# Paired groups of a graph layer: permuting message inputs in float32r instead of permuting f32 message rows

## The reference

```
h    = relu(layernorm(x))
msg  = concat(h[dst], edge_attr)                  # 53125 x 128
m    = relu(msg @ W1a.T + b1a) @ W1b.T + b1b
agg  = segment_sum(m, src) / max(count, 1)        # 3125 x 64
z    = relu(concat(h, agg) @ W2a.T + b2a) @ W2b.T + b2b
out  = x + concat(z, h) @ Wr.T + br
```

## Time and profile before

| | |
|---|---|
| median of 3 runs | 522.39 us (520.93 to 524.32) |
| profiled execution, first to last instruction | 518.3 us |
| median less span | 4.1 us, the start and end that the trace doesn't show |
| PE, DVE, ACT, POOL busy | 431.0, 298.0, 285.0, 356.1 us |
| indirect transfers issued by POOL | 300 + 64 |
| first and last of them | 14.06 us, 477.08 us |

### The profile page before, as it was taken

One profiled execution on the slowest core, in us unless ns is written; L12 is line 12 of the kernel. 1 busy time (PEld: TensorE's weight loads), 2 busy tenths in 40 slices (PEclk: granted clock), 3 DMA queues, 4 the chain that ended last, 5 costly groups with the idle time before them and its releaser, 6 DMA issues.

```text
span 518.3 us, 9203 instructions
## 1 busy us (share of the span) xinstructions
PE 431.0 (83%) x3133; PEld 390.0 (75%) x3133; DVE 298.0 (57%) x825; ACT 285.0 (55%) x576; POOL 356.1 (69%) x406
## 2 busy tenths in 40 slices
PE   6655988899999999998689779845999787987795
PEld 4555777888796988878578778845998777987674
DVE  7868642534656657555425547414765537667884
ACT  3442957774787777786658378171633772100073
POOL 4777777777677777777777777777777777776000
PEclk9876696987999899988899889986999897999999
DMA  7998998553959477978553989996999997778631
GB/s 182 306 338 229 257 266 271 155 156 108 303 143 294 141 257 265 257 255 263 164 151 92 336 249 333 312 331 196 360 326 336 328 322 221 248 214 256 177 86 43
DMA packets 62319, 123.45 MB, mean 238 GB/s; under 512 B 9369, under 2 KB 33374, under 8 KB 62270
## 3 DMA queue, kind: packets, MB, share of 16 engines
q1 hardware_dynamic: 49598, 91.25, 59.0%
q0 software_dynamic: 12672, 31.58, 18.8%
HBM read 71.53 MB, written 51.25 MB: 237 GB/s over the span
## 4 chain that ended last, share of the span: by engine, by line
POOL 32%; PE 26%; DMA 13%; issue 13%; DVE 7%; ACT 5%; SPq 2%; POOLq 0%; ACTq 0%; DVEq 0%
POOL slots_dram L568 24%; PE bank L1261 10%; POOL pairs_dram L551 8%; DMA slots_dram<-pay,pos_i 7%; PE bank L1241 4%; PE bank L1270 4%; DMA dstb<-in_dst 4%; DVE oh L774 2%; DMA rows<-slots_dram 2%; ACT eo L1059 2%; SPq L475 1%; PE bank L1294 1%; PE bank L1291 1%; PE bank L1211 1%; PE bank L1362 1%
## 5 line engine op out<-in xcount | busy, mean ns | idle before, releaser
L568 POOL DMA_INDIRECT slots_dram<-pay,pos_i x300 | 289.0, 963 | 98.7 <-issue 89.6
L1261 PE MATMUL bank<-rows,oh 128*125 128x130 f32 x1100 | 139.5, 287 | 40.3 <-DVE oh L774 40.1
L1261 PEld LDWEIGHTS bank<-rows,oh 128*125 128x125 f32 x1100 | 133.3, 198 | 44.6 <-issue 43.4
L1059 ACT ACTIVATE eo<-dstb,minus_lane 64x256 f32<-64x256 int32 x190 | 85.1, 494 | 94.5 <-DMA dstb<-in_dst 79.8
L1241 PE MATMUL bank<-pw,eo 128*128 128x128 f32 x856 | 119.9, 299 | 3.5 <-ACT pay L1042 2.3
L1241 PEld LDWEIGHTS bank<-pw,eo 128*128 128x128 f32 x856 | 113.3, 213 | 11.4 <-issue 8.0
L774 DVE TENSOR_TENSOR oh<-bank,rows 128x1500 f32<-128x1500 f32 (+5 forms) x67 | 81.8, 1223 | 17.6 <-DMA rows<-slots_dram 10.4
L1270 PE MATMUL bank<-hid,xch 116*128 116x131 f32 (+1 forms) x512 | 68.3, 294 | 14.6 <-DVE xch L724 8.6
L1270 PEld LDWEIGHTS bank<-hid,xch 116*128 116x128 f32 (+1 forms) x512 | 65.3, 205 | 16.9 <-issue 9.9
L551 POOL DMA_INDIRECT pairs_dram<-pay,pos_c x64 | 61.5, 960 | 22.3 <-issue 18.0
L1064 ACT ACTIVATE eo<-eo,one 64x512 f32<-64x512 f32 x95 | 68.3, 719 | 3.1
(11 more groups left out here) (198 smaller groups left out, 376.7 us busy)
## 6 DMA issues: line engine op xcount, KB each, us to landing
rows<-slots_dram SPq DMA_DIRECT2D x24, 864.0 KB
dstb<-in_dst SPq DMA_DIRECT2D x54, 256.0 KB, 7.7
eo<-in_edges_T SPq DMA_DIRECT2D x54, 256.0 KB, 4.9
rows<-pairs_dram SPq DMA_DIRECT2D x12, 864.0 KB
slots_dram<-zeros SPq DMA_DIRECT2D x9, 756.0 KB, 9.2
slots_dram<-pay,pos_i POOLq DMA_INDIRECT x300
rows<-slots_dram SPq DMA_DIRECT2D x8, 432.0 KB
rows<-slots_dram SPq DMA_DIRECT2D x16, 216.0 KB
```

Of the source, the lines that this page charges most:

```text
L568: pool.indirect_dma_start(out=slots_dram[:, :], out_offset=bass.IndirectOffsetOnAxis(ap=pos_i[:, u, k:k + 1], axis=0), in_=pay[:, u, k, :] ...
L1059: last = A.activation(eo[p, g % EB, a * HB:(a + 1) * HB], dstb[p, g % DB // 2, a * HB:(a + 1) * HB], ACT.Square, bias=minus_lane[p, g // 2 ...
L1261: last = T.matmul(o[0:BN, v * SW:(v + 1) * SW], oh2[:, r % 2, n, :], rows[:, sum_no[r] % RR, n, 0:SW], start=(t == 0), stop=(t == TB[ph] - ...
```

## The change

In a paired group nothing goes through `hidden` any more. Instead:

- SP loads the edge features of the group lane by lane (`edges_rows`, 116 x 512 floats, 237 KB) to `staged`; the 256 KB `dstb` broadcast, the `eo` load and the ACT one-hot of a paired group are gone.
- ACT rounds them to float32r (`round_features` to `x_hi`); DVE (`features`) writes mark, destination and a one-hot of `dst` over 62 nodes into `x_hi`, and the remainders to `x_lo`.
- DVE makes the slot one-hots by two instructions of 116 x 1024 a group instead of eight of 116 x 256.
- PE multiplies: stationary `x_hi` and `x_lo`, moving `perm`, all float32r, 16 matmuls of 256 columns a group, in two rounds "perm" of 8.
- ACT copies each half (`copy_moved`, 128 x 512) to `moved`; PE then makes the message rows of two edges per slot from it (`paired_hidden`, 8 f32 matmuls of 131 columns); ACT applies relu into `pay2` (`relu_unit`, 4 of 128 x 262).
- `pos_c` is read from `pay2` as before, at a later point of DVE's list (`places_due`).
- `chunk_marks` and `late_lanes` also clear `x_lo` and `pwx`, and set some columns. `check_chunks` moves from after group 53 to the last "crank". The rings of `eo` and `dstb` count ordinary groups only.
- The planner's constants change. Worked out from its loop, the "h", "z" and sum rounds (number of matmuls of the sums) stand behind these groups:

| | before | after |
|---|---|---|
| h | 7:1, 8:2, 11:1, 12:3 | 7:1, 8:2, 9:2, 10:2 |
| z | 12:2, 15:1, 19:1, 23:1, 27:2 | 11:4, 12:3 |
| sums | 16:24, 20:24, 24:24, 28:12, 31:16, 36:24, 39:12, 40 to 48: 208, 49:6 | 16:24, 18:12, 19:24, 20:12, 22:12, 23:16, 36:24, 38:12, 39 to 47: 208, 48:6 |
| sums at 50 to 53, left over, tail | 100, 75, 25 | 100, 75, 25 |
| perm of c0, c1, c2, c3 | 9, 10, 13, 14 | 8, 9, 12, 13 |

Rounds of a paired group stand ahead of the others in its `after[g]`. The number of scatters, pairs, buckets and slots is the same.

```diff
+LEADS = dict(O=25, C=29)
-    ROUNDS_FROM, FULL_FROM, EARLY_SHARE, SHARE, C_SHARE, MOST = 7, 10, 10, 23, -8, 32
+    ROUNDS_FROM, FULL_FROM, EARLY_SHARE, MOST = 7, 10, 10, 32
+    SHARES = dict(OO=23, CO=11, OC=14, CC=0)
-        units = [("perm", C_GROUPS.index(g - 1), u, 0) for u in range(UNITS)] if g - 1 in C_GROUPS else []
+        if g in C_GROUPS:
+            for half in range(2):
+                after[g].append(len(rounds))
+                rounds.append(("perm", C_GROUPS.index(g), half, 0))
...
+                V.memset(x_lo[:].bitcast(f32), 0.0)
+                link(V.memset(pwx[:], 0.0))
...
+            def features(c):
+                dve.wait_ge(S["xhi"], c + 1)
+                V.tensor_copy(hi[:, :, e + SEEN], mark[0:TILE_A, g, :])
+                link(V.tensor_copy(hi[:, :, e + SEEN + 1], dest))
+                V.tensor_tensor(lo[:, :, e + SEEN + 1], dest, hi[:, :, e + SEEN + 1].bitcast(f32), ALU.subtract)
+                V.tensor_tensor(hi[:, :, e:e + SEEN], marks_all[0:TILE_A, e:e + SEEN].unsqueeze(1).to_broadcast((TILE_A, K, SEEN)),
+                                dst_x[0:TILE_A, pair, lanes].unsqueeze(2).to_broadcast((TILE_A, K, SEEN)), ALU.is_equal)
+                V.tensor_tensor(lo[:, :, edges_in(c)], staged[:, c % XR], hi[:, :, edges_in(c)].bitcast(f32), ALU.subtract).then_inc(S["xp"], 1)
...
+                V.tensor_tensor(perm[:, n % PR], slots_near[0:TILE_A].unsqueeze(1).to_broadcast((TILE_A, 4, 256)),
+                                slot_x[0:TILE_A, c // 2 % 2, k:k + 4].unsqueeze(2).to_broadcast((TILE_A, 4, 256)), ALU.is_equal).then_inc(S["ohp"], 1)
...
+            def copy_moved(r):
+                act.wait_ge(S["ag"], r + 1)
+                A.copy(moved[:, n % 2, :], bank[:, 4 + r % 2, :]).then_inc(S["ep"], 1)
+            def relu_unit(c, u):
+                act.wait_ge(S["H"], part + 1)
+                A.activation(pay2[...], bank[:, part % HIDDEN_BANKS, 0:2 * HW]..., ACT.Relu).then_inc(S["ev"], 1)
...
+            def paired_hidden(c, half):
+                pe.wait_ge(S["ep"], n + 1)
+                for u in (2 * half, 2 * half + 1):
+                    pe.wait_ge(S["ev"], part - HIDDEN_BANKS + 1)
+                    for side in range(2):
+                        last = T.matmul(bank[...], moved[:, n % 2, first:first + 128], pwx[:, c % 2, u, :], start=True, stop=True, ...)
+                    last.then_inc(S["H"], 1)
...
                 elif kind == "perm":
-                            last = T.matmul(o[:, side * HW:(side + 1) * HW], perm[0:n, perm_no[r] % PR, ...],
-                                            hid[0:n, c % HR, 2 * u + t, 0:HW], start=(t == 0), stop=(t == 1), ...)
+                    for u in range(2):
+                        for part in (x_hi, x_lo):
+                            for t, lanes in enumerate((TILE_A, TILE_B)):
+                                last = T.matmul(o[:, 256 * u:256 * u + 256], part[0:lanes, c % XR, 4 * half + 2 * u + t, :],
+                                                perm[0:lanes, n % PR, 2 * u + t, :], ...)
...
+                        if r in last_perm:
+                            paired_hidden(last_perm.index(r), 0)
+                            paired_hidden(last_perm.index(r), 1)
```

More of the change, by code:

```diff
@@ L165, in gnn_layer @@
     round_of = {n: r for r, n in sum_no.items()}
-    first_round = [min(r for r, v in enumerate(rounds) if v[0] == "sum" and v[1] == ph) for ph in range(NPH + 1)]
-    last_perm = [rounds.index(("perm", c, UNITS - 1, 0)) for c in range(len(C_GROUPS))]
+    first_round = [min(r for r, v in enumerate(rounds) if v[0] == "sum" and v[1] == ph) for ph in range(NPH + NCP)]
+    perm_rounds = [[rounds.index(("perm", c, half, 0)) for half in range(2)] for c in range(len(C_GROUPS))]
+    last_perm = [halves[1] for halves in perm_rounds]
     def last_touch(r):
@@ L222, in gnn_layer @@
         col_stat = sb("col_stat", [NBK, 2, 2])
-        beside = sb("beside", [1, 2, 2, 2, NP * 2])
         beside_by = sb("beside_by", [1, 4])
@@ L344, in scatters_of @@
         def scatters_of(u, n):
-            return 16 * sum(KT[O_GROUPS[a]] for a in range(u, n, PB))
+            return 16 * sum(KT[O_GROUPS[a]] for a in range(u, min(n, len(O_GROUPS)), PB))
         def chunk_scatters_of(u, c):
@@ L678, in late_lanes @@
                 V.memset(one[:], 1.0)
+                link(V.tensor_scalar(place_one[:], place[:], 1.0, None, ALU.add))
+                V.tensor_scalar(near_c[:], lane[:], place_one[:], None, ALU.subtract)
                 V.tensor_scalar(minus_lane[:], lane[:], -1.0, None, ALU.mult).then_inc(S["ml"], 1)
@@ L872, in _ @@
                     ranks_b(j)
-                if 2 * i + 1 < ACT_FROM:
-                    onehot(2 * i + 1)
+                if j is not None and 2 * j + 1 < ACT_FROM:
+                    onehot(2 * j + 1)
                 if i == 0:
@@ L895, in _ @@
                     ranks_a(j + 1)
-                if 2 * i + 2 < ACT_FROM:
-                    onehot(2 * i + 2)
+                if j is not None and 2 * j + 2 < ACT_FROM:
+                    onehot(2 * j + 2)
                 rounds_after(2 * i + 1)
-            check_chunks()
+            places_due()
             for r in left_over:
@@ L1106, in _ @@
                     late_weights()
-                for r in after[g]:
-                    if rounds[r][0] == "perm":
-                        copy_unit(r)
-                if ACT_FROM <= g + EB < NG:
-                    onehot(g + EB)
+                if g in O_GROUPS and g + 1 in C_GROUPS:
+                    round_features(C_GROUPS.index(g + 1))
+                if g + EB in O_GROUPS and O_GROUPS.index(g + EB) >= ACT_FROM:
+                    onehot(O_GROUPS.index(g + EB))
             def mean(q):
@@ L1305, in _ @@
                 for g in (2 * i, 2 * i + 1):
-                    hidden(g)
+                    if g >= LG:
+                        continue
+                    if j is not None:
+                        hidden(g)
                     if g % 2 == 0 and 0 < i < NP - 1:
@@ L1433 @@
     edges_T[:, real] = edges[lanes[real]].T
+    paired = [g for g in range(EP // 1024) if ORDER[g // 2] == "C"]
+    edges_rows = edges_T.reshape(D, -1, 8, 128).transpose(1, 3, 2, 0)[paired].reshape(len(paired), 128, 8 * D)
     blocks = dstp.reshape(-1, 512)
```

523 lines of the change are left out of this document (308 added, 215 removed).

## The result

The changed kernel took 541.47 us (median of 4 runs, 536.99 to 544.19) against 522.77 us of the kernel before (4 runs, 520.93 to 524.32): ratio 1.0369, 95% interval 1.0293 to 1.0444. The forecast was 529.9, its range ended at 538. The sign was right, the forecast loss was two fifths of what came (7.5 of 18.7 us).

What follows compares the result with a forecast made beforehand. POOL's transfer pace was taken as the bound. The profiled 518.3 us plus 8.4 delay at c3 less 0.9 for the check gave 525.8; the median's 4.1 above the span made it 529.9 us, range 518.5 to 538.

Steps and rivals of the forecast that it cites:

- What bounds the kernel: POOL's 364 transfers at 1.263 us each set the time from 14 to 478 us; other engines only feed it.
- At most 2.8 + 0.9 us to win: Largest possible gain: 2.8 us of POOL's waits at c2 and c3, 0.9 us of the removed check on DVE.
- The sum to c3: Step-by-step PE and DVE times at full clock from c0 on; c3's scatter starts at 140.2, 5.6 us later.
- D: POOL's delay at c3, carried once to the end: 5.6 us plus 2.8 for low clock, 8.4 us.
- I charge one such group: One paired group up to c3 runs at PE's low clock: paired_hidden 1.8 us more, float32r about 1.0, together 2.8.
- c3 sets it: Behind c3 no group adds delay: c7 ready 6 us later, 2 us late by POOL's old clock, less than D.
- the string saves about 1 us in each of 7 groups: A paired group's chain of DVE, PE and ACT steps takes about 1 us less, in 7 groups up to c7.
- The end: From POOL's last scatter to the end: as before less the check, 39.4 us.
- POOL stays fed: Rival, chance 0.15: c3 ready by 134.3 us, so waits and check are gained; 518.7 to 521.5, about 520 us.
- A small delay: Rival, chance 0.22: PE keeps full clock through h and z, c1 to c3, only 5.6 us added: 527.1 us, down to 522.
- float32r is no cheaper: Rival, chance 0.04: float32r costs as much as f32, 5.7 us more per paired group on PE: 550 to 575 us.
- the end gets shorter: Rival, chance 0.06: group 47's scatters land sooner than 5.7 us, left-over sums 2 to 3 us earlier: about 516.5 us.

Runs made afterwards that it cites:

- z_behind_c15_again: rounds_late with DVE's constants made in its wait at 60 us, their load on SP at group 8, and the z moved behind c15: 519.82 us, ratio 0.9989.
- z_after_c3_again: The changed kernel with only the three z between c2 and c3 moved, to groups 14 and 15: 535.81 us, ratio 1.0263.
- sums_as_before_again: The changed kernel with only the sum matmuls laid out as in the kernel before: 538.16 us, ratio 1.0273.
- pe_filler: The changed kernel with ten dead bf16 matmuls on PE ahead of each paired group: 537.94 us, ratio 1.0275.
- before_early_rounds: The kernel before with the changed kernel's layout of h, z and sum rounds, nothing else: 569.47 us, ratio 1.0959.
- rounds_late: The changed kernel with h spread over groups 7 to 27, z from 27 to 38, sums as before: 524.19 us, ratio 1.0053.

## Why the prediction was wrong, by its steps

The path was right: POOL is the clock and c3 is where most is lost. Three terms were too small: the time to c3 (the low clock charged to one group, and c0's ranks put 3.1 us late where they came 6.4 late), the delay behind c3 (put at nothing) and the end (put down as before).

*What bounds the kernel.* Right, and it carried the whole analysis: POOL's pace held (0.30 us between transfers in every run but those on the two other chips), PE's busy time fell and nothing was won, and POOL's waits added up to the delay of its last scatter. "At most 2.8 + 0.9 us to win" was not exceeded: without any wait behind the first `z_behind_c15_again` is level with the kernel before. The 0.9 us of the check were subtracted from an end that came out longer; no run shows them by themselves.

*float32r and DVE's pieces.* 0.122 us against 0.11 forecast; one-hots 1.22 and 1.22; memsets 1.76 and 0.93 against 1.75 and 0.9.

*The sum to c3.* Its order of events was right, each step came late. When PE was through with the step (us):

```
                      forecast   measured   late by
c_carry of c0           74.3       77.6       3.3
c0                      87.5       91.5       4.0
two h, c1               97.8      102.3       4.5
h h                    101.8      106.1       4.3
group 11, ranks        112.2      117.4       5.2
z z z z                120.1      125.3       5.2
c2                     127.0      132.8       5.8
c3                     139.3      146.1       6.8
```

So D at c3 was 12.65 us and not 8.4. 3.3 of the 7.0 us that the full-clock sum lacked were there before c0: `hidden(7)` at the low clock (3.76 us instead of 2.03) and DVE's constants (`eq` 4.37 us later, not 3.3). The rest stands where the clock was low: group 11's hidden (3.29 instead of 1.95) and the permutations of the paired groups. The step that failed here is "I charge one such group", 2.8 us: four ran low, and so did two `hidden` that the charge didn't look at. Its parts were off too: a permutation cost 3.4 instead of 1.95 us, 1.5 more and not 1.0, `paired_hidden` 0.1 to 0.4 more and not 1.8. In five executions with the four `z` in this place (the changed kernel, `z_after_c3_again`, `sums_as_before_again`, `pe_filler`, `before_early_rounds`) the clock fell between 120.3 and 123.5 us with PE busy ahead of it and behind it; that the `z` are the cause is not shown, since `rounds_late` has a low c2 without them. That the `h` and `z` are what c3 pays was right, and the layout was priced at 8.5 us where moving it costs 15.3 in the kernel before and 18.9 between the changed kernel and `rounds_late`. In part these are more rounds than the 8.5 us counted: the two `h` ahead of c0 in the kernel before filled a time in which PE waits for DVE's ranks; behind c0 they fill nothing (c1 3.7 us later in `before_early_rounds`).

*"c3 sets it."* c3 sets 12.65 of 16.47 us; that nothing comes behind it was wrong. D grew to 15.65 at c7. From c3's ready time to c7's the kernel before took 56.8 us and the changed one 63.7, where POOL needs 48 x 1.263 = 60.6; the difference to POOL is those 3 us. The step that failed is "the string saves about 1 us in each of 7 groups": PE waited 33.4 us for DVE's one-hots in 14 places over the sixteen groups. DVE works `h`, `z` and sums off in between; which of these makes the wait was not told apart. c7 was ready 19.5 us later than before (191.1 to 210.6), where the prediction had 6.

*The end.* Forecast 39.4 us behind the last scatter, measured 43.6. On the chips of 522 us it is 40.7 to 43.6 in all variants of the changed kernel and 39.2 to 41.9 in those of the kernel before. The failed step is that the end was put down as before, less the check. In the changed kernel's own trace a part is clock (0.83 from 497 to 517 us, before 1.00 up to 507) and group 47's landing (6.64 against 5.70). What makes the rest was not tried and stays open, and so do the 8 ns more per transfer.

Together: 4.25 at c3, 3.8 behind it, 4.2 in the end make the 12.3 us between 525.8 and 538.1. The first two alone would have come to just under 538 us by the forecast's sum (529.9 + 4.25 + 3.8), the edge of the range; it had no room for the third.

*The rivals.* "POOL stays fed" had its deciding point right (c3 ready by 134.3) and is what `rounds_late` shows, at 524.19 us and so without the gain. "A small delay" fell: c3 was late by more than 5.6 us and all four permutations ran at the low level. The clock didn't hold through the four `z`: it fell at 120.8 us in the middle of them. "float32r is no cheaper" fell with 0.122 us a matmul, "the end gets shorter" with group 47's landing in 6.64 us instead of 5.70.

## What to carry to other kernels

Where one engine issues at a fixed pace, ask of each group when it was ready, not only how long was waited for it: the waits of the issuing engine add up to the delay of the end, but a group that was ready in time shows none, whether it had 4.1 us in hand (c7 in the kernel before) or 0.4 (c1). Work that an in-order engine does "in between" has no price of its own; it has that of its place, from nothing where the engine waits anyway to more than its own length where the next group is due and another engine must take it up first. A change that saves an engine time and reorders its filler in one go should be measured in both parts: here PE was relieved of 11.5 us (431.0 to 419.5) where POOL was the clock, and taking the new order back alone won 14.7 us of the median.
